# A two-layer message-passing network on one core: windows of 24, 44, 62 or 80 columns in place of 80, and a loop cut in three

## The reference, cut to what matters

```python
msg = concatenate([x[src], edge_attr]) @ W_msg.T
agg = segment_sum(msg, dst)          # sum over the edges that arrive at a node
x   = gru_cell(agg, x)               # two small matrix products, sigmoids, a tanh
```

## Time and profile before

| | us |
|---|---|
| median of 3 runs (lowest, highest) | 3264.28 (3263.8, 3271.02) |
| the profiled execution's own time | 3276.25 |
| its span in the trace | 3274.5 |
| POOL busy | 2327.7 |
| PE busy | 2628.8 |
| DVE busy | 1530.2 |
| granted clock of PE, mean | 0.835 of full speed |

### The profile page before, as it was taken

How to read it: one execution, slowest core, us unless ns; L and a number is a source line. 1 busy time by engine, 2 the same in 40 slices (tenths; PEclk the granted TensorE clock), 3 DMA queues, 4 the chain that set the end, 5 groups by cost and what they waited for, 6 DMA issues and landing times.

```text
span 3274.5 us, 74397 instructions
## 1 busy us (share of the span) xinstructions
PE 2628.8 (80%) x20375; PEld 2358.9 (72%) x20376; DVE 1530.2 (47%) x4895; ACT 998.9 (31%) x2344; POOL 2327.7 (71%) x2390
## 2 busy tenths in 40 slices
PE   0779889889898898898966677787777787788787
PEld 0678778778787787787855667676777677687675
DVE  5645454545454554545433434443444444444443
ACT  5222223223233232332431222232222232333333
POOL 4577777777777676767717777777777777777772
PEclk9978888889798897988986777787777787887888
DMA  7233333333333333333315222222222222222221
GB/s 195 70 84 92 86 90 91 88 89 92 83 96 83 85 94 80 88 80 85 85 43 116 54 55 58 55 61 58 58 59 60 59 65 57 64 62 60 64 63 39
DMA packets 350922, 249.44 MB, mean 76 GB/s; under 512 B 226506, under 2 KB 312334, under 8 KB 350628
## 3 DMA queue, kind: packets, MB, share of 16 engines
q0 software_dynamic: 75232, 155.02, 17.5%
q1 hardware_dynamic: 254617, 70.47, 10.2%
q10 hardware_dynamic: 20779, 20.48, 2.1%
HBM read 226.51 MB, written 19.20 MB: 75 GB/s over the span
## 4 chain that ended last, share of the span: by engine, by line
PE 34%; POOL 32%; issue 16%; DVE 6%; DVEq 4%; DMA 3%; ACT 2%; ACTq 1%; SPq 1%; POOLq 1%
POOL rows L670 32%; PE ps_v L766 9%; PE ps_win L806 7%; PE ps_win L790 4%; PE ps_q L759 3%; DVEq L1192 2%; PE ps_c L759 2%; PE ps_b L883 1%; PE ps_b L884 1%; DVEq L1222 1%; PE ps_d L870 1%; PE ps_d L899 1%; ACT hr L1371 1%; PE ps_a L890 1%; DVE rel L1132 1%
## 5 line engine op out<-in xcount | busy, mean ns | idle before, releaser
L670 POOL DMA_INDIRECT rows<-h_table,idx x1156 | 1153.5, 998 | 475.1 <-issue 379.6
L670 POOL DMA_INDIRECT rows<-x_table,idx x1156 | 1146.8, 992 | 410.6 <-issue 401.4
L806 PE MATMUL ps_win<-onehot,rows 128*128 128x80 f32 x4624 | 743.6, 312 | 217.3 <-DMA rows<-x_table,idx 175.6
L806 PEld LDWEIGHTS ps_win<-onehot,rows 128*128 128x128 f32 x4624 | 663.5, 221 | 263.8 <-issue 154.6
L766 PE MATMUL ps_v<-hr,a_blk 125*128 125x128 f32 x4800 | 713.9, 318 | 0.0
L766 PEld LDWEIGHTS ps_v<-hr,a_blk 125*128 125x128 f32 x4800 | 697.4, 234 | 0.6
L1393 ACT COPY a_blk<-ps_q 125x224 f32<-125x224 f32 (+5 forms) x504 | 223.8, 480 | 850.9 <-PE ps_q L759 798.6
L1120 DVE SCALAR_TENSOR_TENSOR v_hot<-v_cur,lane 128x42 bf16<-128x42 f32 (+13 forms) x1180 | 435.1, 425 | 0.0
L790 PE MATMUL ps_win<-onehot,attr 128*64 128x80 f32 x3128 | 311.8, 252 | 115.3 <-DVE onehot L1135 76.3
L759 PE MATMUL ps_q<-v_hot,lo_hot 128*125 128x28 bf16 (+5 forms) x3696 | 288.1, 221 | 139.2 <-DVE v_hot L1120 117.2
L759 PEld LDWEIGHTS ps_q<-v_hot,lo_hot 128*125 128x125 bf16 x3696 | 271.4, 151 | 150.2 <-DVE v_hot L1120 128.5
(11 more groups left out here) (193 smaller groups left out, 2044.4 us busy)
## 6 DMA issues: line engine op xcount, KB each, us to landing
attr<-in_edge_attr_dram SPq DMA_DIRECT2D x390, 128.0 KB
rows<-h_table,idx POOLq DMA_INDIRECT x1156
rows<-x_table,idx POOLq DMA_INDIRECT x1156
dst_in<-in_dst_dram SPq DMA_DIRECT2D x678, 2.0 KB
idx<-in_src_dram SPq DMA_DIRECT2D x576, 2.0 KB
x_table<-out_sb ACTq DMA_DIRECT2D x50, 125.0 KB
attr<-in_x_dram ACTq DMA_DIRECT2D x50, 125.0 KB
out_dram<-out_sb ACTq DMA_DIRECT2D x50, 125.0 KB
```

The lines of the kernel that those rows point to most:

```text
L670: nc.gpsimd.indirect_dma_start(out=rows[0:parts, s, j, :], out_offset=None, in_=table[:, :], in_offset=bass.IndirectOffsetOnAxis(ap=idx[0: ...
L806: mm = nc.tensor.matmul(ps_win[r % 2][:, 0:WIN], rows[0:parts, rr, j, :], onehot[0:parts, r % 2, j, :], start=(j == 0), stop=(j == TILES - 1))
```

## The change

The width of a group's window now follows its place in the list. `class_widths` gives the attribute groups 24 columns, the gathered groups of iterations 0 to 3 44, those of 4 to 7 62, and those of 8 to 11 and the rest 80 as before. The width reaches the one-hot (DVE), both kinds of matmul (PE) and the window's additions (DVE). Because a width must be a constant in an instruction, PE and DVE get three loops of 4 iterations for each layer in place of one of 12; the body is written out three times. POOL, ACT and SP keep their loops. In the preparation, DVE adds `80 - w` to the spans of the narrower groups (three more instructions), so that the test for groups that reach too far stays right.

```diff
+ATTR_WIN = 24
+PARTS_OF_LIST = ((0, 4, 44), (4, 8, 62), (8, 12, WIN))
...
+            for a, b, w in class_widths():
+                if w < WIN:
+                    ins = nc.vector.tensor_scalar(spans[:, a:b], spans[:, a:b], float(WIN - w), None, ALU.add)
+            chained(ins)
...
-                def attr_sums(r, parts):
+                def attr_sums(r, parts, w):
                     for j in range(TILES):
-                        mm = nc.tensor.matmul(ps_win[r % 2][0:D, WIN:2 * WIN], attr[0:parts, r, j, :],
-                                              onehot[0:parts, r % 2, j, :], start=(j == 0), stop=(j == TILES - 1))
+                        mm = nc.tensor.matmul(ps_win[r % 2][0:D, WIN:WIN + w], attr[0:parts, r, j, :],
+                                              onehot[0:parts, r % 2, j, 0:w], start=(j == 0), stop=(j == TILES - 1))
...
-                        mm = nc.tensor.matmul(ps_win[r % 2][:, 0:WIN], rows[0:parts, rr, j, :],
-                                              onehot[0:parts, r % 2, j, :], start=(j == 0), stop=(j == TILES - 1))
+                        mm = nc.tensor.matmul(ps_win[r % 2][:, 0:w], rows[0:parts, rr, j, :],
+                                              onehot[0:parts, r % 2, j, 0:w], start=(j == 0), stop=(j == TILES - 1))
...
-                with pe.Fori(0, ITERS) as it:
-                    blk = block_of(layer, it)
+                for it_from, it_to, width in PARTS_OF_LIST:
+                    with pe.Fori(it_from, it_to) as it:
+                        blk = block_of(layer, it)
...
-                        onehot[:, s % 2, :, :],
-                        lane[:, 0:WIN].unsqueeze(1).to_broadcast([P, TILES, WIN]),
-                        rel[:, s % 2, :].unsqueeze(2).to_broadcast([P, TILES, WIN]), ALU.is_equal).then_inc(onehot_ready, 1)
+                        onehot[:, s % 2, :, 0:w],
+                        lane[:, 0:w].unsqueeze(1).to_broadcast([P, TILES, w]),
+                        rel[:, s % 2, :].unsqueeze(2).to_broadcast([P, TILES, w]), ALU.is_equal).then_inc(onehot_ready, 1)
...
-                        e = edgeT[0:D, bass.ds(base, WIN)]
-                        ins = nc.vector.tensor_tensor(e, e, ps_win[s % 2][0:D, WIN:2 * WIN], ALU.add)
+                        e = edgeT[0:D, bass.ds(base, w)]
```

More of the change, by code:

```diff
@@ L903, in _ @@
                         attr_group(p, p % AR, p // AR)
-                with pe.Fori(0, ITERS) as it:
-                    blk = block_of(layer, it)
[L906 to L919, removed]
-                            else:
[L921 to L927, removed]
@@ L929, in _ @@
+                group(TAIL[layer], TAIL[layer] % AR, 0, REST, WIN, TAIL[layer] // AR, gather_use(layer, ITERS, 0))
                 overflow(pe, over_body)
@@ L1346, in _ @@
-                add_window(TAIL[layer], FULL, TAIL[layer] % AR, REST, True)
+                for it_from, it_to, width in PARTS_OF_LIST:
+                    with dve.Fori(it_from, it_to) as it:
+                        blk = block_of(layer, it)
+                        for q, gi, ai in order(layer):
+                            g = it * ATTR + ai if gi is None else gathered(it, gi)
+                            add_window(place(layer, it, q), g, slot(layer, q), ATTR_WIN if gi is None else width, gi is not None)
+                            onehot_after(it, it_to, width, q)
+                            if gi == USED:
+                                add_block(it, blk, place(layer, it, q + 1))
+                            if gi is not None and gi < USED:
+                                sl, phase = divmod(gi, 3)
+                                if phase == 0:
+                                    for k in range(2, PACKS):
+                                        if sl == 0:
+                                            lo_pack(it, k)
+                                        pack_of(blk, sl, k)
+                                elif phase == 2 and sl + 1 < SLICES:
+                                    for k in range(2):
+                                        pack_of(blk, sl + 1, k)
+                                elif phase == 2:
+                                    for k in range(2):
+                                        lo_pack(it + 1, k)
+                                        pack_of(blk + 1, 0, k)
+                                elif sl == SLICES - 1:
+                                    prepare(it + 1)
+                                    nc.vector.tensor_scalar(v_onehot[:, :], lane[0:VC, :], vrel[:, bass.ds(it, 1)], None,
+                                                            ALU.is_equal).then_inc(v_hot_made, 1)
+                            last = q + 1 == len(order(layer))
+                            if last or (gi is not None and gi % RING == RING - 1 and gi + 1 < SLOTS):
+                                u = SUBS - 1 if last else gi // RING
+                                ready_chunks(dve, it * SUBS + u, chunk)
@@ L1347, in _ @@
+                add_window(TAIL[layer], FULL, TAIL[layer] % AR, WIN, True)
                 added_before(TAIL[layer] + 1)
```

115 lines of the change are left out of this document (56 added, 59 removed).

## The result

The changed kernel takes 3286.53 us (median of 5 runs, 3280.72 to 3290.02), against 3264.28 us (3263.8 to 3271.02) before. The ratio is 1.0051, with a 95% interval of 1.0037 to 1.0065: about 17 us, half a per cent, slower (the two medians alone lie 22 us apart). The forecast was 3273 us, 9 us slower. The profiled execution took 3287.22 us with a span of 3285.5 us and a mean granted clock of 0.802 (0.835 before). That fall is in every execution: 0.802 to 0.804 in the five of the changed kernel, 0.830 to 0.839 in the 62 of the kernel before that ran beside the experiments.

A forecast was written before the change was run, and what follows sets the result against it. POOL was taken to bound layer 1 and layer 0's iterations 0 to 3, PE layer 0's end, changing hands in 4 to 7. Terms 8 + 12.7 - 11.2 - 2 = +7.5, say +9 us on 3264.28, gave 3273 us, range 3232 to 3304.

The forecast's parts named there:

- Attribute sums: PE, layer 0: narrower sums of eight records save 0.12 us each, 16.1, 15.4 and 3.8 us by four iterations.
- Row sums: PE, layer 0: weights set the pace, so 44 or 62 columns in place of 80 save nothing.
- The clock, iterations 0 to 7: PE, layer 0: clock falls to 0.77 in iterations 0 to 3 and 0.81 in 4 to 7, costing 45 and 40 us.
- Iterations 8 to 11: Layer 0: 11.2 us gained, from the branch's wait (3.4), clock behind it (4) and attribute sums (3.8).
- The loop in three: PE, layer 0: two branches back go, saving 3.4 us each at iterations 3 to 4 and 7 to 8.
- DVE: Layer 0: shorter one-hots cut PE's waits for them by 2 us; the added preparation instructions cost nothing.
- Layer 1: No change, 0 us: POOL keeps its pace of 1.30 us a gather, so a faster PE gives nothing.

The follow-up runs named there:

- e5: The changed kernel, but PE streams 80 columns in attribute sums and 100 in row sums, DVE still narrow: 3231.54 us, 0.9878 of the kernel before.
- e4: The changed kernel with DVE's one-hots and PE's attribute sums back at 80 columns, only PE's row sums narrow: 3292.55 us, 1.0080 of the kernel before.
- e1: The changed kernel with all widths back at 80, so only the three loops on PE and DVE remain: 3285.35 us, 1.0044 of the kernel before.
- e7: The kernel before, all widths 80, with three loops of 4 iterations on DVE alone, PE's loop whole: 3282.95 us, 1.0042 of the kernel before.
- e6: The kernel before, all widths 80, with three loops of 4 iterations on PE alone, DVE's loop whole: 3271.82 us, 1.0009 of the kernel before.
- e3: The changed kernel with DVE's one-hots back at 80 columns, PE's sums and DVE's additions still narrow: 3298.57 us, 1.0090 of the kernel before.
- e2: The changed kernel with PE streaming 80 columns in every sum, DVE's one-hots and additions still narrow: 3254.97 us, 0.9954 of the kernel before.
- e9: The kernel before with its one loop and DVE at 80, PE's row sums at 100 columns: 3255.81 us, 0.9960 of the kernel before.
- e10: The kernel before, one loop, with attribute groups' one-hots and additions 24 wide on DVE and PE's row sums at 100: 3251.83 us, 0.9951.
- e8: The kernel before, one loop, with attribute groups' one-hots and additions 24 wide on DVE, PE at 80 columns: 3264.44 us, 0.9986.
- e12: The kernel before, all widths 80, with DVE's loop cut at iterations 1 and 2, PE's loop whole: 3267.6 us, 0.9996 of the kernel before.

## Why the prediction came out right, step by step

The forecast named a slower clock as what eats the gain, and that is what happened. That its sum came near the measured time is luck: errors of 10 us and more cancel in it.

*Attribute sums:* right. 11 ns a record at the full clock, 25 at the lower one: 0.09 and 0.20 us a sum, 0.12 taken. The records are 55 to 60 ns apart, as said.

*Row sums:* right, nothing. 1.03 to 1.07 us for eight at 62, 80 and 100 columns. The Trainium skill ("TensorE: Matmul & The Clock Gate", section "Back-to-back issue gap") lets an isolated gap grow with the columns; in this stream it does not, with 128 x 128 f32 weights.

*The clock, iterations 0 to 7:* right in size. 0.77 and 0.81 taken; measured 0.765 (0.81 over 128 us and 0.75 over 379) and 0.81. PE's busy time grew by 31 us in iterations 0 to 3 (+29 taken) and by 15 in 4 to 7 (40 - 15.4, so +25, taken). Iterations 0 to 3 came 9 us later (+8 taken), 4 to 7 took 10 us more (+12.7 taken); in part that is luck too, since the 10 us hold the loss of DVE's loop (below), which the forecast did not have. The Trainium skill (same page, section "Why this matters for your kernels") ties a fall in mid-kernel to idle gaps. By that rule the change would have been free. Here the clock fell more often while PE's waits went from 150 to 118 us, half of the falls came with no idle stretch over 1 us ahead, and more columns raised it (e5); the trace speaks against using the rule alone.

*Iterations 8 to 11:* this step failed. I took -11.2 us (the branch's wait, 4 us of clock behind it, and the attribute sums) and measured +6 (549 against 543). The +6 itself is not clear of noise: e4, e1 and e7, which all stream 80 columns in these iterations, took 548, 543 and 537 us. The gain of 11 us is what did not come. Four stretches of the changed kernel: from the start of iterations 4, 8 (two pieces) and 9.

```profile
616.00:633.00 17.00, 17.00 (x109) 16.38 (x107) 7.37 (x23) 3.69 (x8) 13.04 (x14) 0.53 0.30 74
1147.00:1155.00 8.00, 5.50 (x60) 4.82 (x59) 5.57 (x13) 3.90 (x8) 6.17 (x7) 0.93 0.31 80
1155.00:1162.00 7.00, 6.84 (x41) 6.60 (x42) 3.06 (x13) 0.64 (x2) 5.48 (x6) 0.58 0.28 72
1284.00:1301.00 17.00, 17.00 (x101) 16.36 (x100) 7.76 (x22) 3.69 (x8) 10.99 (x11) 0.50 0.25 64
```

Iteration 8 does start without the wait at the branch, at 0.93. But 8 us later the clock is 0.58, a fall that only moved: PE waits 1.63 and 1.02 us for DVE's `v_hot` just ahead of it. At iteration 4 nothing came back: 0.53 over 17 us, since PE still waits 4.67 us for a one-hot just ahead of it. And e6, which has both branches removed on PE and nothing else, is no faster than before. The 3.4 us twice and the 4 us of clock were waits taken off that brought the kernel nothing.

*The loop in three:* missed wholly. I held it for a gain, 3.4 us twice and 4 us of clock, and looked only at PE; on DVE it costs 0.42%, about 14 us.

*DVE:* mis-sized. I took 2 us from PE's waits for one-hots. Narrow one-hots are worth 0.39% (e3 to after), 12 us, where PE is narrow, and with the narrow additions 0.90% (e1 to e2), 30 us, where PE streams 80 columns. Part of it is layer 1 (below), which I had at nothing.

*Layer 1:* I took 0, at POOL's constant pace. In the profiles, the time from layer 1's first gather to its last fell from 1500.3 to 1489.1 us; the gathers got shorter. Before, and after:

```profile
L670 POOL DMA_INDIRECT rows<-h_table,idx x1156 | 1153.5, 998 | 475.1 <-issue 379.6
L670 POOL DMA_INDIRECT rows<-x_table,idx x1156 | 1146.8, 992 | 410.6 <-issue 401.4
```

```profile
L680 POOL DMA_INDIRECT rows<-h_table,idx x1156 | 1137.7, 984 | 516.0 <-issue 370.0
L680 POOL DMA_INDIRECT rows<-x_table,idx x1156 | 1136.4, 983 | 409.3 <-issue 399.6
```

9 ns x 1156 = 10 us. This paid back two fifths of the 24.7 us by which layer 1's first gather came later in the trace. Not all of it is the widths': in e1, with 80 columns everywhere, the gathers of layer 1 take 987 ns.

In ratios, with the parts added in this order, the change is: three loops +0.44%, narrow DVE -0.90%, narrow PE +0.97%, together +0.51%. (With PE made narrow first it is +0.44%, +0.46% and -0.39%.) The forecast had narrow PE at +20 us (8 + 40 - 15.4 - 8.5 - 3.8), about two thirds of the 31.6 us measured; the loops at -11 us where they cost 14; and DVE at -2 us where it gave 12 to 30. The last two errors have opposite signs, and that is why the sum fits.

## What to carry to other kernels

In this kernel the records of the row sums are paced by their weights (eight take 1.02 us at 44 columns and 1.06 to 1.07 at 100): there the moving columns are free in time, and what they do is hold the clock up. In such a place narrow what DVE computes, and leave what PE streams wide, or widen it with columns that nobody reads. Measure the length of the records first. Before you count the removal of a wait as a gain, look at what else is late at that moment (here DVE's one-hot), and count a loop that is cut on every engine whose program it changes, not on the waiting one alone.

## What the runs showed of the hardware that was not expected

*Columns hold the clock.* With DVE's work and the order of the instructions the same, time at the lower clock in layer 0's loop was 583 us with narrow streams (after), 425 with 80 columns (e2), 345 with 100 in the row sums (e5). The falls that differ are those without an idle stretch over 1 us ahead (28, 8 and 1 of them); of the others there are 27, 30 and 29. Wider row sums were not tried. What the chip counts, columns or something that goes with them, isn't told apart; e5 and e9 also move the attribute sums within the accumulator and widen and clear the one-hot buffer, which was not tried alone; e1 to e4, which move nothing, show the same dependence between narrow and 80.

*POOL's indirect gathers are shorter where DVE's one-hots are narrow.* Layer 0's take 995 to 1000 ns in all eight kernels whose one-hots are 80 wide, 991 and 993 with the attribute groups narrow (e10, e8), and 984 to 988 in the four with all narrow. In layer 1 it is 985 to 992 against 980 to 983. The Trainium skill ("SBUF — State Buffer", section "SBUF: two separate sides") says that VectorE and GpSimd share a pair of ports, which one of them holds for a whole instruction, and that a VectorE operation with two inputs from SBUF can be such a case, against a GpSimd operation that reads SBUF. That would fit, by its sign; no run here shows the ports or whether a gather's issue reads SBUF in that way, and 5 to 12 ns of 990 is an average that doesn't tell a few long holds from many short ones.

*A cut in DVE's loop moved PE's clock* (e7: ratio 1.0042, clock 0.824 to 0.828; e12, cut at other iterations: 0.9996, 0.832 to 0.838). It is a reminder that 0.4% of this kernel can come from where the falls of the clock lie, and that a difference of that size needs a control with the code's new shape and the old work.
